# Expert mask in a transformer block: multiplied by GpSimd instead of added by selector matmuls

## The chip, the cores and the metric

One core of one Trainium2 chip runs the whole kernel in one launch. The metric is the device time of one execution, in microseconds (us). Lower is better. TensorE (PE) does matmuls, VectorE (DVE), ScalarE (ACT) and GpSimd (POOL) do the elementwise work, and SyncE (SP) issues all DMA transfers of this kernel.

## What is computed

For each of 4 sequences ("rows", `b`) of 1024 tokens with 256 features, the input is normalised per token (`xn`). Causal attention with 16 heads of 16 features, with rotary positions, and a feed-forward layer are both computed from `xn`, and both are added to the input. The feed-forward layer keeps, for each token, the 4 of 16 blocks of 64 hidden units that a router scores highest:

```python
prob = softmax(xf @ router_w.T + router_b)
_, idx = top_k(prob, 4)
mask = zeros((n, 16), bool).at[arange(n)[:, None], idx].set(True)
h = einsum('nd,ibd->nib', xf, w1b) + b1b
h = relu(where(mask[:, :, None], h, 0))
y = einsum('nib,dib->nd', h, w2b) + b2
return x + attention(xn) + y.reshape(x_shape)
```

## The kernel before

**Tiling.** Tokens lie in 8 tiles of 128 (`NT`), features in 2 blocks (`KB`), hidden units in 8 blocks of 128 (`FB`, each two router blocks). Attention runs in 16 groups of 4 heads (`GROUPS`, 4 for each row). A group has 48 "maxima" (a bfloat16 matmul of scores at L1065, whose maximum VectorE takes at L1333 and L1336), then 48 "scores" (L1124, with the causal triangle at L1127), whose exponentials ScalarE takes (L941), and 12 products with the values (`pv`, L1140). Maxima run about one group ahead of scores. GpSimd splits the maxima into three bfloat16 pieces (`split_maxima`, L832 to L841), TensorE transposes them (`maxT`, L1072), and SyncE places them through DRAM (`place_maxima`, L678 and L680) under the queries.

**The feed-forward layer.** It works on quarters of 256 tokens. For each hidden block, `hidden` runs two float32 matmuls (L1040, each recorded as two instructions) and a third, bfloat16 one (L1044). That third one multiplies a constant `sel` (-1e30 where a hidden unit belongs to a router block) by `unselT`, the transposed mask of blocks not chosen, so that ReLU on ScalarE (L932) with the bias gives zero there. `hT` holds one quarter, so the ReLU of the next quarter waits for the output tiles of this one. `ffn_tile` (L1053) multiplies `hT` by `w2` in two halves of four hidden blocks, and waits before each block, for even tiles, for ScalarE's count. VectorE adds the tile to `acc` (L1351). The mask comes from `route_logits` and `route_top` on VectorE, 8 transposes (L1032) and a copy (L1322).

**The order of work.** `arrange()` is a planner that runs when the kernel is built. It keeps a clock in TensorE columns, the moments when 7 PSUM banks come free, and costs of each work (`COST`, `READ`, `CHORE`, `POOL`). It lays out `ORDER` for TensorE, and from it the orders of ScalarE, VectorE and `POOL_ORDER` for GpSimd. Each engine runs its list strictly in order. `FIRST` is a fixed start for row 0. `group_work` says which feed-forward and projection works are spread over which group, in the order in which they must run, and a work that isn't due lets maxima or scores go first. GpSimd's list holds the rotations and splits into pieces of q and k (`CHAIN`: sin, cos, add, high, rest, mid, low; L786 to L814), the splits of maxima (which go first), the normalising of x (L820) and the addition of biases (L847).

**SyncE's queue** is written out by hand: loads of inputs, stores of pieces (L632, L639, L655), loads of "stacks" of pieces for a group (L647, L669), placements of maxima, stores and loads of attention outputs (L690, L701), and stores of results. A wait in it holds all that stands behind it.

**The last output weights.** The last group of the last row isn't sent over DRAM: `last_out` (L1112) multiplies `o_norm` by `wo_last`, the output weights of 4 heads laid 32 partitions apart, which four DMAs (L709) put into a buffer that VectorE set to zero (L1420).

## Time and profile before

| | |
|---|---|
| time, median of 3 runs | 830.44 us (830.43 to 831.54) |
| time of the profiled execution | 829.97 us |
| its span in the trace | 828.1 us |
| TensorE busy | 809.9 us, 98% |
| VectorE busy | 579.3 us, 70% |
| ScalarE busy | 426.2 us, 51% |
| GpSimd busy | 281.5 us, 34% |
| data moved by DMA | 81.9 MB, mean 99 GB/s |

The span runs from the first to the last instruction of the trace; the time of the execution includes what lies around it. Busy time of TensorE has overlaps merged: matmuls are pipelined, so the duration of one is longer than the distance between the starts of two. Releasers in brackets are inferred from semaphores. "L12" is line 12 of the kernel.

### The profile page before, as it was taken

Reading aid. Unit: us, or ns where it says so; the run is one execution under the profiler, and the core shown is the slowest. Engines: PE = TensorE matmul, PEld = TensorE weight load, DVE = VectorE, ACT = ScalarE, POOL = GpSimd, SP = SyncE. Lnnn points to the kernel's source line nnn. Section 1 sums busy time; section 2 is a strip of 40 time slices with the busy share of each in tenths; the row PEclk is TensorE's granted clock in tenths of the full one; section 3 lists DMA queues with packets and bytes.
Section 4 is the critical chain, followed back from the end, with each engine's and each line's share of the span. In section 5 each row is a group of like instructions: output and inputs, shape, how many; then the busy total and the mean of one; then the engine's idle time right before and its main releaser. Section 6 shows DMA issues by size and latency. Waiting matters only on the chain.

```text
span 828.1 us, 14880 instructions
## 1 busy us (share of the span) xinstructions
PE 809.9 (98%) x5278; PEld 492.0 (59%) x5278; DVE 579.3 (70%) x1799; ACT 426.2 (51%) x1018; POOL 281.5 (34%) x299
## 2 busy tenths in 40 slices
PE   5999999999999999999999999999999999999998
PEld 3677454544556655656656556664766556465764
DVE  6969877777998767576786856667676776767312
ACT  2523545665645645555464554645465464546552
POOL 3495149343650159067041028508400002000000
PEclk9999999999999999999999999999999999999999
DMA  8862515232524354141333315232060425000011
GB/s 273 243 186 77 169 53 166 92 90 92 147 73 125 94 142 151 43 118 39 87 133 74 95 53 166 91 91 92 2 215 4 109 61 142 15 15 16 15 58 51
DMA packets 53335, 81.91 MB, mean 99 GB/s; under 512 B 6796, under 2 KB 22092, under 8 KB 53260
## 3 DMA queue, kind: packets, MB, share of 16 engines
q1 hardware_dynamic: 53260, 80.95, 32.2%
q8 instruction: 42, 0.69, 0.4%
q14 instruction: 33, 0.27, 0.1%
HBM read 43.06 MB, written 37.88 MB: 98 GB/s over the span
## 4 chain that ended last, share of the span: by engine, by line
PE 92%; DVE 4%; ACT 2%; issue 1%; DMA 1%; SPq 0%; ACTq 0%; DVEq 0%
PE o_bank L1140 16%; PE banks L1065 14%; PE banks L1124 14%; PE banks L1040 14%; PE banks L1053 14%; PE banks L1014 7%; PE banks L1127 3%; PE banks L1023 3%; PE banks L1092 3%; PE banks L1044 2%; ACT probs L941 2%; DVE part_max L1333 1%; PE banks L1004 1%; DVE o_norm L1370 1%; DVE o_bank L1363 1%
## 5 line engine op out<-in xcount | busy, mean ns | idle before, releaser
L941 ACT ACTIVATE probs<-banks 128x512 f32<-128x512 f32 (+3 forms) x768 | 328.0, 496 | 244.0 <-PE banks L1127 174.5
L1124 PE MATMUL banks<-q_st,k_st 99*128 99x512 bf16 (+3 forms) x768 | 234.7, 327 | 2.6 <-ACT probs L941 1.0
L1065 PE MATMUL banks<-k_st,q_st 96*128 96x512 bf16 (+3 forms) x768 | 228.7, 327 | 0.7 <-DVE part_max L1333 0.2
L1336 DVE CUSTOM_DVE_ANT_0 banks<-banks,tri,part_max 128x512 f32<-128x512 f32 (+3 forms) x256 | 129.0, 555 | 68.3 <-PE banks L1065 68.0
L1333 DVE TENSOR_REDUCE part_max<-banks 128x1 f32<-128x512 f32 x256 | 160.1, 679 | 17.6 <-PE banks L1065 17.1
L1336 DVE CUSTOM_DVE_ANT_0 banks<-banks,tri 128x512 f32<-128x512 f32 (+3 forms) x256 | 120.1, 516 | 34.3 <-PE banks L1065 33.4
L832 POOL TENSOR_SCALAR max_neg<-row_max 128x16 f32<-128x16 f32 x32 | 8.1, 253 | 382.6 <-DVE row_max L1336 382.6
L1040 PE MATMUL banks<-xnT,w_sb 128*128 128x256 f32 x512 | 134.5, 386 | 0.1
L1140 PE MATMUL o_bank<-probs,v_sb 128*17 128x512 f32 (+3 forms) x1536 | 133.2, 487 | 0.7 <-DVE o_norm L1370 0.7
L1053 PE MATMUL banks<-w_sb,hT 128*128 128x256 f32 x512 | 121.2, 383 | 0.0
L1065 PEld LDWEIGHTS banks<-k_st,q_st 96*128 96x128 bf16 x768 | 73.3, 98 | 73.9 <-issue 19.9
L1124 PEld LDWEIGHTS banks<-q_st,k_st 99*128 99x128 bf16 x768 | 74.6, 97 | 61.4 <-ACT probs L941 18.1
L1127 PE MATMUL banks<-identb,tri 128*128 128x128 bf16 x512 | 108.1, 219 | 0.0
L1053 PEld LDWEIGHTS banks<-w_sb,hT 128*128 128x128 f32 x512 | 94.5, 190 | 16.7 <-ACT rope_sb L918 0.4
L1040 PEld LDWEIGHTS banks<-xnT,w_sb 128*128 128x128 f32 x512 | 90.7, 189 | 23.1 <-issue 2.8
L932 ACT ACTIVATE hT<-banks,b_sb 128x256 f32<-128x256 f32 x128 | 60.6, 474 | 81.7 <-PE banks L1044 68.7
L1140 PEld LDWEIGHTS o_bank<-probs,v_sb 128*17 128x17 f32 x1536 | 40.4, 97 | 87.0 <-issue 65.4
L1336 DVE DVE_READ_ACCUMULATOR2_ANT row_max<- 128x1 f32 x512 | 72.2, 141 | 0.0
L1127 PEld LDWEIGHTS banks<-identb,tri 128*128 128x128 bf16 x512 | 50.3, 98 | 18.8 <-issue 0.7
L1363 DVE STREAM_TRANSPOSE o_bank<-o_bank 128x512 f32<-128x512 f32 x31 | 22.7, 734 | 41.4 <-PE o_bank L1140 41.3
L1351 DVE TENSOR_TENSOR acc<-acc,banks 128x256 f32<-128x256 f32 x32 | 13.5, 421 | 46.2 <-PE banks L1053 46.2
L786 POOL TENSOR_TENSOR rope_sb<-rope_sb,sin_sb 128x1024 f32<-128x1024 f32 x14 | 33.0, 2357 | 34.7 <-DVE rope_sb L1272 34.7
(97 smaller groups left out, 732.5 us busy)
## 6 DMA issues: line engine op xcount, KB each, us to landing
term_scratch<-pieces SPq DMA_DIRECT2D x84, 256.0 KB, 2.9
q_st<-term_scratch SPq DMA_DIRECT2D x16, 768.0 KB, 5.9
k_st<-term_scratch SPq DMA_DIRECT2D x16, 768.0 KB, 8.3
y_scratch<-o_norm SPq DMA_DIRECT2D x31, 256.0 KB, 2.0
acc<-in_x SPq DMA_DIRECT2D x8, 512.0 KB, 3.9
rope_sb<-y_scratch SPq DMA_DIRECT2D x15, 256.0 KB
out<-acc SPq DMA_DIRECT2D x7, 512.0 KB, 2.9
x_sb<-in_x SPq DMA_DIRECT2D x3, 1024.0 KB, 5.8
```

The lines of the kernel that those rows point to most:

```text
L786: nc.gpsimd.tensor_tensor(y2, y2, sin_sb[:], ALU.mult).then_inc(rotated, 1)
L932: nc.scalar.activation(hT[:, m, :], filled("hid", b, q, m)[:, 0:QTR], ACT.Relu, bias=b1_sb[:, m:m + 1]).then_inc(s_out, 1)
L941: nc.scalar.activation(probs[:, h, PROBS_AT[u]:PROBS_AT[u] + w], filled("score", n, k, h)[:, 0:w], ACT.Exp, scale=SCALE).then_inc(s_out, 1)
L1014: last = nc.tensor.matmul(bank, w[:, k, mb * P:(mb + 1) * P], xnT[:, b % 2, k, c * HALF:(c + 1) * HALF], start=(k == 0), stop=(k == KB - 1))
L1040: nc.tensor.matmul(bank[:, 0:QTR], w1_sb[:, k, m * P:(m + 1) * P], xnT[:, b % 2, k, tokens], start=(k == 0), stop=False)
L1053: last = nc.tensor.matmul(bank[:, 0:D], hT[:, m, t % 2 * P:(t % 2 + 1) * P], w2_sb[:, m, :], start=(m == 0), stop=(m == FB - 1))
L1065: nc.tensor.matmul(bank[:, 0:w], q_st[0:KROWS, at, h, i * P:(i + 1) * P], k_st[0:KROWS, at, h, c * HALF:c * HALF + w], start=True, stop=Tr ...
L1124: last = nc.tensor.matmul(bank[:, 0:w], k_st[0:SROWS, at, h, j * P:(j + 1) * P], q_st[0:SROWS, at, h, q0:q0 + w], start=True, stop=not dia ...
L1127: last = nc.tensor.matmul(bank[:, 0:P], tri_k, identb[:], start=False, stop=True)
L1140: last = nc.tensor.matmul(o_bank[h * OW:h * OW + VW, q0:HALF], v_sb[:, b % 2, j, g * GH + h, :], probs[:, h, PROBS_AT[u]:PROBS_AT[u] + HAL ...
L1333: ins = nc.vector.tensor_reduce(part_max[:, h, at:at + 1], bank[:, 0:w], AX.X, ALU.max)
L1336: ins = nc.vector.tensor_tensor_reduce(bank[:, 0:w], bank[:, 0:w], tri[:, HALF - w:HALF], 1.0, least, ALU.add, ALU.max, to)
```

## The change

The selector matmul and its constant go. The mask is now that of the chosen blocks (1 or 0), transposed by the same 8 transposes (`chosenT`), copied by VectorE and stored to DRAM (`store_chosen`). `load_gates` reads it back for a quarter by two DMAs, each spreading 8 rows of the mask over 64 partitions, into `gates`, double buffered. After each two hidden blocks GpSimd multiplies the ReLU's output in place by the gates (`gate`), 64 times in all. `ffn_tile` waits for that instead of for ScalarE. The planner gets the cost of a gate (2700 columns), gives it priority behind the splits of maxima, and orders an output tile only when its gates are done by its clock. The first rotations of row 0 move from a fixed place into the planner's list. In SyncE's queue the stores and loads of gates are put between others. `wo_last` becomes one array, built beforehand, that is loaded into `x_sb`, the input buffer, after the last row's transposes.

```diff
-COST = {"hid": 2 * 4 * QTR + QTR, ...
+COST = {"hid": 2 * 4 * QTR, ...
...
+GATED, GATES = 500, 20000
+POOL = {"gate": 2700, "split": 3600, ...
...
-            todo = min(able, key=lambda todo: todo[1][0] != "split")
+            todo = min(able, key=lambda todo: ("split", "gate").index(todo[1][0]) if todo[1][0] in ("split", "gate") else 2)
...
+    def work_ready(what):
+        return what[0] != "ffn" or gated.get((what[1], what[2] // 2, 2 * what[3] + 1), clock + 1) <= clock
+
     def do_work(works):
         what = works.pop(0)
+        while not work_ready(what):
+            clock += 50
+            pump()
...
+        if what[0] == "chosenT":
+            gates[what[1]] = ready["vector"] + GATES
+        elif what[0] == "hid" and what[3] % 2:
+            pool_work(max(ready["scalar"], gates.get(what[1], 0)), ("gate", what[1], what[2], what[3] // 2))
...
-    pool_work(clock + 40000, *((step, 0, r) for r in (2, 3) for step in CHAIN[3:]))
+    pool_free = clock
+    pool_work(clock, *((step, 0, r) for r in (2, 3) for step in CHAIN[:3]))
+    pool_work(clock + 15000, *((step, 0, r) for r in (2, 3) for step in CHAIN[3:]))
...
-                may_work = works and may_fill(works[0][0])
+                may_work = works and may_fill(works[0][0]) and work_ready(works[0])
...
+            def store_chosen(b):
+                if b >= 2:
+                    for buffer in range(2):
+                        sp.wait_ge(gates_in[buffer], (b - 1) * 2 * 32)
+                sp.wait_ge(m_out, M_COUNT["chosenT", b])
+                sp.dma_start(gate_scratch[b % 2], chosenT[:]).then_inc(chosen_out, 16)
+
+            def load_gates(b, q):
+                if b or q >= 2:
+                    sp.wait_ge(gated, (b * 4 + q - 1) * FB // 2)
+                if q == 0:
+                    sp.wait_ge(chosen_out, (b + 1) * 16)
+                tokens = slice(q * QTR, (q + 1) * QTR)
+                for i in range(2):
+                    rows = gate_scratch[b % 2].rearrange("(m i) t -> i m t", i=2)[i, :, tokens]
+                    sp.dma_start(gates[i * 64:(i + 1) * 64, q % 2], rows.partition_broadcast(64)).then_inc(
+                        gates_in[q % 2], 16)
...
-            for h in range(GH):
-                d = (H - GH + h) * HD
-                sp.dma_start(wo_last[h * OW:h * OW + HD, :], woT[d:d + HD, :]).then_inc(wo_last_in, 16)
             load_x(1)
             store_first_pieces(0)
             store_first_pieces(1)
             load_first_stack()
+            store_chosen(0)
+            load_gates(0, 0)
+            load_gates(0, 1)
             store_other_pieces(0)
             store_other_pieces(1)
             load_stacks(1)
             place_maxima(0, 0)
+            load_gates(0, 2)
             store_pieces(0, 2)
             for b in range(B):
...
                 place_maxima(n, 1)
                 if b == 0:
+                    load_gates(0, 3)
...
                 place_maxima(n + 1, 0)
                 if b:
+                    store_chosen(b)
+                    load_gates(b, 0)
+                    load_gates(b, 1)
                     store_out(b - 1, 0)
...
+                elif not more:
+                    sp.wait_ge(s_out, S_COUNT["xnT", B - 1, NT // 2 - 1])
+                    sp.dma_start(wo_last, wo_last_c).then_inc(wo_last_in, 16)
                 place_maxima(n + 1, 1)
+                if b:
+                    load_gates(b, 2)
...
                 place_maxima(n + 2, 1)
+                if b:
+                    load_gates(b, 3)
...
+            def gate(b, q, pair):
+                pool.wait_ge(s_out, S_COUNT["hid", b, q, 2 * pair + 1])
+                if pair == 0:
+                    pool.wait_ge(gates_in[q % 2], (b * 2 + q // 2 + 1) * 32)
+                blocks = slice(2 * pair, 2 * pair + 2)
+                nc.gpsimd.tensor_tensor(hT[:, blocks, :], hT[:, blocks, :], gates[:, q % 2, blocks, :],
+                                        ALU.mult).then_inc(gated, 1)
...
-                if q == 0 and m == 0:
-                    pe.wait_ge(m_out, M_COUNT["unselT", b])
-                nc.tensor.matmul(bank[:, 0:QTR], sel[:, m, :], unselT[:, tokens], start=False,
-                                 stop=True).then_inc(s_fill, 1)
...
-                    if t % 2 == 0:
-                        pe.wait_ge(s_out, S_COUNT["hid", b, t // 2, m])
+                    if t % 2 == 0 and m % 2 == 0:
+                        pe.wait_ge(gated, (b * 4 + t // 2) * FB // 2 + m // 2 + 1)
```

## Rows read from the trace of the kernel before

**Rows 1.** The page: busy us and share of each engine; the chain by engine.
```profile
PE 809.9 (98%) x5278; PEld 492.0 (59%) x5278; DVE 579.3 (70%) x1799; ACT 426.2 (51%) x1018; POOL 281.5 (34%) x299
...
PE 92%; DVE 4%; ACT 2%; issue 1%; DMA 1%; SPq 0%; ACTq 0%; DVEq 0%
```
**Rows 2.** Windows: length, busy us of PE, PEld, DVE, ACT, POOL; clock, DMA share, GB/s.
```profile
0.00:50.00 50.00, 40.62 (x171) 28.17 (x172) 36.70 (x125) 19.86 (x46) 24.65 (x14) 1.00 0.83 259
50.00:100.00 50.00, 49.47 (x284) 32.88 (x281) 43.05 (x147) 19.92 (x46) 22.85 (x27) 1.00 0.44 128
100.00:200.00 100.00, 98.10 (x645) 49.15 (x644) 76.82 (x228) 55.23 (x127) 53.94 (x49) 1.00 0.34 105
...
300.00:400.00 100.00, 99.87 (x650) 61.10 (x649) 66.22 (x190) 51.05 (x117) 56.10 (x48) 1.00 0.30 91
```
**Rows 3.** A selector matmul and its successor in time: start, us, line.
```profile
61.12 0.27 PE L1044 MATMUL banks<-unselT,sel 128*128 128x256 bf16 x1
61.23 0.81 PE L1065 MATMUL banks<-k_st,q_st 96*128 96x512 bf16 x3
```
**Rows 4.** GpSimd's operations by line: ns min/median/max; or busy us, mean ns.
```profile
L786 POOL TENSOR_TENSOR rope_sb<-rope_sb,sin_sb x14: 2346/2356/2375, 43.0 to 574.3; 128x1024 f32<-128x1024 f32 x14
...
L808 POOL TENSOR_TENSOR rope_sb<-rope_sb,pieces 128x1024 f32<-128x1024 f32 x14 | 29.8, 2132 | 1.1
...
L820 POOL TENSOR_SCALAR x_sb<-x_sb,mv,rstd 128x256 f32<-128x256 f32 x24 | 28.9, 1220 | 38.1 <-DVE rstd L1251 38.1
```
**Rows 5.** L1044's waits (us, times); DMAs to landing, the last is L678's.
```profile
  DVE unselT L1322: 2.1, 3
...
k_st<-term_scratch SPq DMA_DIRECT2D x16, 768.0 KB, 8.3
...
acc<-in_x SPq DMA_DIRECT2D x8, 512.0 KB, 3.9
...
DMA to landing us min/median/max: 1.3/1.8/5.3
```
**Rows 6.** Ends of two quarters, all engines, in order of time.
```profile
425.58 9.65 POOL L820 TENSOR_SCALAR x_sb<-x_sb,mv,rstd 128x256 f32<-128x256 f32 x8 [20.03 <-DVE rstd L1251]
...
433.55 0.47 ACT L932 ACTIVATE hT<-banks,b_sb 128x256 f32<-128x256 f32 x1 [0.30 <-PE banks L1044]
...
436.08 1.94 PE L1053 MATMUL banks<-w_sb,hT 128*128 128x256 f32 x8
...
796.65 0.53 ACT L932 ACTIVATE hT<-banks,b_sb 128x256 f32<-128x256 f32 x1
...
797.02 3.62 PE L1053 MATMUL banks<-w_sb,hT 128*128 128x256 f32 x16
```
**Rows 7.** The start of the first quarter's output, all engines, in time.
```profile
37.83 0.68 DVE L1322 COPY unselT<-banks 16x1024 bf16<-16x1024 bf16 x1 [0.42 <-PE banks L1032]
...
38.69 0.27 PE L1044 MATMUL banks<-unselT,sel 128*128 128x256 bf16 x1
...
43.00 2.36 POOL L786 TENSOR_TENSOR rope_sb<-rope_sb,sin_sb 128x1024 f32<-128x1024 f32 x1
...
45.63 1.03 PE L1065 MATMUL banks<-k_st,q_st 96*128 96x512 bf16 x4
...
46.16 0.70 DVE L1336 CUSTOM_DVE_ANT_0 banks<-banks,tri 128x512 f32<-128x512 f32 x1 [5.15 <-PE banks L1065]
...
46.49 1.89 PE L1053 MATMUL banks<-w_sb,hT 128*128 128x256 f32 x8
```
**Rows 8.** Row 1: a placing of maxima on SyncE; the first output tile.
```profile
266.91 0.73 SPq L680 DMA_DIRECT2D q_st<-max_scratch  x1
...
301.20 1.99 PE L1053 MATMUL banks<-w_sb,hT 128*128 128x256 f32 x8
```
**Rows 9.** VectorE's cosine product beside a GpSimd copy, in time.
```profile
25.23 0.41 POOL L857 COPY o_norm<-bv_sb 128x256 f32<-128x256 f32 x1
...
25.30 0.88 DVE L1281 TENSOR_TENSOR rope_sb<-rope_sb,cos_sb 128x512 f32<-128x512 f32 x1
```

More of the change, by code:

```diff
@@ L206 @@
 SPLIT, PLACE = 1200, 16000
-POOL = {"split": 3600, "sin": 5640, "cos": 5640, "add": 5640, "high": 2500, "rest": 5100, "mid": 2500,
+GATED, GATES = 500, 20000
+POOL = {"gate": 2700, "split": 3600, "sin": 5640, "cos": 5640, "add": 5640, "high": 2500, "rest": 5100, "mid": 2500,
         "low": 5100, "xn": 1580, "bias": 5700}
@@ L246, in pump @@
                 split[todo[1][1:]] = pool_free + SPLIT
+            elif todo[1][0] == "gate":
+                gated[todo[1][1:]] = pool_free + GATED
     def engine_of(kind):
@@ L323, in do_work @@
                 do_max()
-            order.append(works.pop(0))
+            what = works.pop(0)
+            while not work_ready(what):
+                clock += 50
+                pump()
+            order.append(what)
             clock += COST["ffn"]
             read(what, at, READ["ffn"])
+            wide = True
             return 2 * COST["ffn"]
         read(what, fill(what, COST[what[0]]), READ[what[0]])
+        if what[0] == "chosenT":
+            gates[what[1]] = ready["vector"] + GATES
+        elif what[0] == "hid" and what[3] % 2:
+            pool_work(max(ready["scalar"], gates.get(what[1], 0)), ("gate", what[1], what[2], what[3] // 2))
         if what[0] == "out" and what[1] + 1 < B and what[2] % 2:
@@ L392, in arrange @@
             do_max()
-        elif works:
+        elif works and work_ready(works[0]):
             do_work(works)
@@ L489, in block_kernel @@
         tri_k = tri[:, HALF - P:HALF]
[L490 removed]
+        gates = sb("gates", [P, 2, FB, QTR], BF16)
         pieces = sb("pieces", [P, 2, NPIECE, T], BF16)
@@ L1039, in hidden @@
                 for k in range(KB):
-                    nc.tensor.matmul(bank[:, 0:QTR], w1_sb[:, k, m * P:(m + 1) * P], xnT[:, b % 2, k, tokens],
-                                     start=(k == 0), stop=False)
-                if q == 0 and m == 0:
-                    pe.wait_ge(m_out, M_COUNT["unselT", b])
-                nc.tensor.matmul(bank[:, 0:QTR], sel[:, m, :], unselT[:, tokens], start=False,
-                                 stop=True).then_inc(s_fill, 1)
+                    last = nc.tensor.matmul(bank[:, 0:QTR], w1_sb[:, k, m * P:(m + 1) * P], xnT[:, b % 2, k, tokens],
+                                            start=(k == 0), stop=(k == KB - 1))
+                last.then_inc(s_fill, 1)
             def ffn_tile(b, t, part):
@@ L1108, in last_out @@
                 if i == 0:
-                    pe.wait_ge(wo_last_in, 16 * GH)
+                    pe.wait_ge(wo_last_in, 16)
                 if i % 2 == 0:
                     pe.wait_ge(normed, 2 * GROUPS + i // 2)
-                nc.tensor.matmul(banks[:, BANK["outl", t], 0:D], o_norm[:, 1, i * P:(i + 1) * P], wo_last[:], start=False,
+                nc.tensor.matmul(banks[:, BANK["outl", t], 0:D], o_norm[:, 1, i * P:(i + 1) * P], wo_last, start=False,
                                  stop=True).then_inc(m_fill, 1)
```

110 lines of the change are left out of this document (53 added, 57 removed).

## Prediction

> **What bounds the kernel now.** I read the busy shares first: TensorE is busy 98% of the span, VectorE 70%, ScalarE 51% and GpSimd 34%, and the chain of work that ended last is 92% TensorE [rows 1]. The windows say where this holds: TensorE is busy 49.5 of 50 us from 50 to 100 us, and 98.1 to 99.9 of every 100 us from 100 to 800 us (the two ends of these seven are shown); only the first 50 us (40.6 busy) and the tail are thinner [rows 2]. The granted clock is 1.00 in all of them, which is the 2.4 GHz level. So nearly every column taken off TensorE after 50 us is time taken off the end, unless its instructions begin to wait for somebody. The other engines have room over a stretch: GpSimd is busy 56 of 100 us in its fullest window, though VectorE has little between 50 and 100 us (43 of 50) [rows 2].
>
> One execution is what I can add up: its span is 828.1 us, and its time was 829.97, so 1.9 us lie around the span. The median of the three runs is 830.44, 0.5 us above it.
>
> **Selector matmuls removed.** There are 128 of them. The 0.27 us that the trace gives one is not its price, because matmuls overlap in the pipeline. The order of time shows it: a selector starts at 61.12 and its successor at 61.23 [rows 3], and so it is for nearly all. That is 0.11 us each; 256 columns at 2.4 GHz are 0.107. 128 x 0.109 = 13.9 us. In 3 places TensorE also waited for the copy of the transposed mask, 2.1 us together [rows 5]; part of this overlaps weight loads, and I count 0.5. Together -14.4 us. The selector's weight load lies under the matmul in front of it and gives nothing. The bracket is 13.7 (columns alone) to 16.0 (all of the wait as well).
>
> **Gate multiplications added on GpSimd.** There are 64, each over 128x512, float32 by bfloat16 into float32. The nearest rows are the subtraction of a bfloat16 piece, 2.13 us for 1024 columns, and the sine product, 2.36 [rows 4]. Their halves are 1.07 and 1.18; with some fixed part I take 1.16. The high end is the scalar-pair operation, 1.22 us for 256 columns [rows 4], which would make 2.44. 64 x 1.16 = 74 us, so GpSimd goes from 281 to about 355 us of 815. As throughput this costs nothing; as a relay between ScalarE and TensorE it can.
>
> How late is each quarter's relay? In 16 quarters of hidden layers, the second half of the first output tile needs the last hidden block. In row 1, quarter 3, the last ReLU ends at 434.02 and the second half starts at 436.08, 2.1 us later [rows 6]. In the last quarter the ReLU ends at 797.18, and eight matmuls of 0.216 after 797.02 the second half starts, 1.6 us later [rows 6]. Read in the same way the distance is 1.6 to 2.8 us in 11 quarters and 7 to 19 in five. (The first half needs only block 3 and had 4.1 us or more.) The new path takes a hand-over from ScalarE and one to TensorE, some 0.24 together (from the mask copy's end at 38.51 to the matmul at 38.69 it was 0.18 [rows 7], and between dependent GpSimd steps 0.06), and the gate's 1.16: 1.4 us. With GpSimd free that fits, and the planner orders an output tile only when its gates are due. With GpSimd inside a rotation step it must wait up to 2.36 us [rows 4]. Laid over the old times, GpSimd is in the last of eight normalising steps until 435.23 in row 1, quarter 3 [rows 6], so a gate would end at 436.4 and the half be 0.5 us late; row 0, quarter 1 would be 1.6 late by a rotation step in the same way, and quarter 2 of rows 1 and 2 would just fit. Since the order moves, I price four such meetings by their mean excess over 0.7 us of slack: 3 x 1.65x1.65/(2x2.36) = 1.7, and 0.1 for the shorter step. I take +2; the bracket is 0 to 6.
>
> **Start-up, the one place where the relay is exposed.** Today the hidden blocks of quarter 0 end at 45.63, four maxima follow, and the first output tile starts at 46.49 [rows 7]. After the change the blocks end at about 44.8. The transposed mask is ready at 38.5 [rows 7]; its store of 32 KB should land like the maxima's store of 12 KB (1.3 to 5.3 us, median 1.8 [rows 5]), at 40.5. Then come the broadcast loads, 512 KB a quarter in rows of 512 bytes. The trace has none; bounds are the acc load of the same size (3.9 us) and the k_st load (8.3 for 768 KB) [rows 5], so they land at 44.9 to 49.3. I take 46, near the lower row, as the size is its own. GpSimd is held until 43.00 by the bias additions and until 45.4 by one rotation step [rows 7]. Two gates from 46 end at 48.3, the first half starts at 48.5, and its second half waits 0.6 us more for the fourth gate. TensorE meanwhile has about 12 maxima (1.9 us of columns; VectorE needs 0.70 us for a wide one [rows 7], so they can't come faster). Idle: 48.5 - 44.8 - 1.9 = 1.8, + 0.6 = 2.4; if a second rotation step goes first, 2.35 more. I take +3, bracket 1.2 to 7.5. This isn't recovered, because TensorE is full from there on and the work is the same.
>
> **SyncE's queue.** Four issues for the last output weights and one for the selector go; 4 stores and 32 loads come, at 0.3 to 0.8 us each. Behind the first five of them stand the 12 stores of the other heads and the stack of group 1, some 4.5 us later than now; the first maxima of group 1 come after all 48 of group 0, each of which takes VectorE 0.3 to 0.9 us, so the cover is some 20 us and nothing is charged. In row 1 the first gates stand behind the placing of maxima, which ends at 267.64, so they land near 275; the first output tile is at 301.20 [rows 8]: 26 us of cover, and GpSimd, which must stand at its first gate until then, had nothing else in its list before 287. A later quarter's load waits for the gates two quarters back, which then come a group's part earlier; behind it stand a stack and a placing that have ten us or more. Cost 0. The extra 16 x 512 KB = 8.4 MB find the DMA engines at a third of their time [rows 2]: 0.
>
> **Last output weights.** They are loaded once, ready-made, into a buffer free since the last transposes, long before their use in the last matmuls. The four head loads and a memset near the start leave, where VectorE waits for x anyway. 0 at both ends.
>
> **GpSimd beside VectorE.** A row shows that they can slow each other: VectorE's cosine product took 0.88 us at 25.30, where a GpSimd copy ran from 25.23 to 25.64 [rows 9], and 0.68 the other three times. It reads two SBUF tensors. In the long middle VectorE reads PSUM with at most one SBUF operand, and GpSimd's 14 sine products took 2346 to 2375 ns whatever VectorE did [rows 4]. So 0. The Trainium skill (GPSIMD Engine Reference, Key points) says that GpSimd shares its SBUF interfaces with VectorE, with contention for VectorE instructions in a 2-port mode or with two SBUF inputs. The trace agrees with both halves of this, and by that rule moving work to GpSimd would cost only in the routing and first rotations, under 1 us here.
>
> **Sum.** 828.1 - 14.4 + 2 + 3 = 818.7 of span, + 1.9 = 820.6. The planner lays the whole order anew; the stretches of 100 us differ in TensorE's idle time by 1.8 us (98.10 to 99.87 [rows 2]), so I give the order -1 to +3 and round to 821.
>
> **Rivals.** (1) *The relay is the new bound, slower than before.* If a gate takes g us, start-up costs 3 + 4(g - 1.16), the ten tight quarters past it (median distance 2.1) cost g + 0.24 - 2.1 each once positive, and the four meetings 2 in sum and 0.8 each more for each us of g above 1.16. At g = 2.44 this is 8.1 + 5.8 + 2 + 4 x 1.0 = about 20, so 829.97 - 14.4 + 20 = 836. It decides from g of about 2.1. For it speaks the scalar-pair row; against it both tensor-pair rows [rows 4]. Chance 0.08. (2) *TensorE's freed time becomes waiting.* VectorE has 43 of 50 us between 50 and 100 [rows 2], GpSimd's splits of maxima now stand behind gates and rotations, and placements arrive later; half or more of the gain goes: 826 to 831, say 828. Against it: from 300 to 400 us TensorE lacks only 0.13 us of its window with VectorE at 66 and ScalarE at 51 [rows 2]. Chance 0.14. (3) *The clock falls in the start-up gap.* The granted clock stayed 1.00 in the first window, where TensorE lacks 9.4 us [rows 2], but no gap of 2 to 5 us after its start exists in this trace. Were the following 5 us at 1.2 GHz, they would deliver half their columns: +2.5, 823.5; with 10 us, +5. The Trainium skill (TensorE: Matmul & The Clock Gate, the part on the clock gate) has the clock depend on how busy TensorE was lately, halved when idle; by it this is possible, and maxima every 0.7 us speak against. Chance 0.06. (4) *The change does not do what it says*, the selectors' columns being hidden: then 830. The starts in [rows 3] nearly exclude this; 0.02.
>
> **How the numbers follow.** The forecast, 821 (815.5 to 826), has 0.70. Low end: 829.97 - 16.0 + 1.2 = 815.2; high: all brackets' upper halves, 826. The range of 8 in 10 takes in rival 3 and most of rival 2: 815 to 829. A measurement here can tell about 0.2% (1.7 us) from no change. Rival 2 splits into 0.09 faster, 0.04 within and 0.01 slower. Faster: 0.70 + 0.06 + 0.09 = 0.85; within: 0.04 + 0.02 = 0.06; slower: 0.08 + 0.01 = 0.09.
>
> **What would show it.** The selector's line is gone, and a hidden block's fourth matmul is followed by its successor after 0.22 us. Gates take 1.1 to 1.2 us. The first output tile starts between 48 and 50, with VectorE's maxima undisturbed. Waits of TensorE for GpSimd appear at quarter ends, under 6 us in sum, with the clock at 1.00. I am wrong if gates take over 2 us, if the first tile starts after 53, or if waits for maxima or their placing grow.

## The result, and the profile after

The changed kernel takes 835.5 us (median of four, 833.7 to 836.3) against 830.9 for the kernel before on the same chip: 1.0054 of its time, with a 95% interval of 1.0042 to 1.0066. I had forecast 821, between 815 and 829. It is slower by 4.5 us where I expected 9.4 less, so 14 us are to be found. The four executions fall in two pairs: 833.7 and 834.8 with a mean granted clock of 0.996, and 836.2 and 836.3 with 0.992; the traced one, from which all rows of this kernel come, is one of the slower pair.

From the page of the changed kernel: busy time of each engine, the chain that ended last by engine, and two groups (busy us, mean ns of one | idle time before them and what ended it).

```profile
PE 807.0 (97%) x5150; PEld 483.2 (58%) x5150; DVE 580.4 (70%) x1798; ACT 424.8 (51%) x1018; POOL 352.9 (42%) x362
PE 88%; ACT 4%; DVE 3%; DMA 2%; POOL 1%; issue 1%; SPq 0%; DVEq 0%; ACTq 0%; POOLq 0%
L877 POOL TENSOR_TENSOR hT<-hT,gates 128x512 f32<-128x512 f32 x64 | 73.7, 1156 | 207.9 <-ACT hT L993 141.1
L1111 PE MATMUL banks<-w_sb,hT 128*128 128x256 f32 x512 | 124.9, 389 | 6.7 <-POOL hT L877 6.7
```

The gates (L877) came out as forecast: 64 of 1.156 us. TensorE still has 88% of the chain, but it had 92 [rows 1], and the difference went to waits and to DMA. The windows say where, against [rows 2]:

```profile
core 0: us, PE busy (x) PEld busy (x) DVE busy (x) ACT busy (x) POOL busy (x), PEclk, DMA share, GB/s
0.00:50.00 50.00, 38.95 (x153) 26.39 (x153) 36.99 (x127) 19.86 (x46) 19.17 (x11) 1.00 0.76 227
50.00:100.00 50.00, 45.66 (x245) 31.77 (x246) 36.46 (x129) 15.22 (x36) 37.52 (x37) 0.90 0.54 146
100.00:200.00 100.00, 96.32 (x599) 48.88 (x597) 76.36 (x216) 54.53 (x126) 55.80 (x53) 0.98 0.38 112
300.00:400.00 100.00, 99.30 (x618) 57.02 (x617) 65.75 (x184) 50.90 (x118) 66.14 (x51) 1.00 0.36 112
```

TensorE's busy time from 50 to 100 us fell from 49.5 to 45.7 and the granted clock from 1.00 to 0.90, so even of the busy time a part ran at half rate. From 100 to 200 a smaller loss of both kinds follows. From 200 us on it is 98.5 to 99.6 of every 100, a little under before.

The start in order of time (start us, us, engine line op out<-in xcount [idle before <-what ended it]):

```profile
36.62 0.59 SPq L671 DMA_DIRECT2D q_st<-term_scratch  x1
38.46 0.32 SPq L671 DMA_DIRECT2D k_st<-term_scratch  x1
38.65 0.68 DVE L1380 COPY chosenT<-banks 16x1024 bf16<-16x1024 bf16 x1 [0.42 <-PE banks L1093]
39.36 0.32 SPq L714 DMA_DIRECT2D gate_scratch<-chosenT  x1
...
45.64 1.68 PE L1123 MATMUL banks<-k_st,q_st 96*128 96x512 bf16 x8
45.77 2.70 SPq L725 DMA_DIRECT2D gates<-gate_scratch  x4
...
48.93 0.28 PE L1123 MATMUL banks<-k_st,q_st 96*128 96x256 bf16 x1 [0.36 <-DVE row_max L1394]
...
52.82 4.49 POOL L877 TENSOR_TENSOR hT<-hT,gates 128x512 f32<-128x512 f32 x4 [6.66 <-DMA gates<-gate_scratch]
...
54.12 3.75 PE L1111 MATMUL banks<-w_sb,hT 128*128 128x256 f32 x8 [4.90 <-POOL hT L877]
...
58.12 0.43 DVE L1394 CUSTOM_DVE_ANT_0 banks<-banks,tri 128x256 f32<-128x256 f32 x1 [6.04 <-PE banks L1123]
```

The mask left VectorE at 39.33 and its store was issued at 39.36. SyncE could issue the loads only when the store had landed, at 45.77: 6.4 us later. Their data released GpSimd at 52.82, 7.0 us later again. The first output tile began at 54.12, where it had begun at 46.49 [rows 7]. TensorE had issued the 11 maxima that its order has ahead of the first tile by 48.93, the last of them at the pace at which VectorE frees banks, and then stood for 4.9 us. VectorE, with nothing new in the banks, stood for 6.04. In windows of 2 us over the same place (columns as above) one sees what the standing did to the clock:

```profile
46.00:48.00 2.00, 1.61 (x9) 0.58 (x6) 1.83 (x5) 0.23 (x1) 0.16 (x1) 1.00 0.12 33
48.00:50.00 2.00, 0.57 (x2) 0.19 (x2) 2.00 (x9) 0.00 (x0) 0.00 (x0) 0.92 0.43 115
50.00:52.00 2.00, 0.00 (x0) 0.00 (x0) 2.00 (x10) 0.00 (x0) 0.00 (x0) 0.50 1.06 209
52.00:54.00 2.00, 0.00 (x0) 0.00 (x0) 0.08 (x2) 0.00 (x0) 1.18 (x2) 0.50 1.17 262
54.00:56.00 2.00, 1.88 (x5) 1.54 (x6) 0.00 (x0) 0.00 (x0) 2.00 (x2) 0.50 1.07 343
56.00:58.00 2.00, 2.00 (x7) 1.44 (x6) 0.00 (x0) 0.00 (x0) 2.00 (x3) 0.50 1.01 308
58.00:60.00 2.00, 2.00 (x7) 1.56 (x6) 0.49 (x2) 0.00 (x0) 1.61 (x1) 0.52 0.15 41
60.00:62.00 2.00, 2.00 (x13) 1.70 (x12) 1.18 (x7) 0.00 (x0) 0.00 (x0) 1.00 0.68 179
```

The granted clock went to 0.50, the 1.2 GHz level, from about 49.7 (the window from 48 to 50 has 0.92) to 60 us. TensorE had been busy 2.2 of the 4 us from 46 to 50 and its last maximum had ended at 49.21, so the clock fell within 0.5 us of the gap's start. Six of those ten microseconds were work at half rate, some 3 us of time (my estimate from these rows). A second, smaller case follows in row 0's last quarter: the last gate stood behind six normalisations of x on GpSimd.

```profile
109.12 7.23 POOL L884 TENSOR_SCALAR x_sb<-x_sb,mv,rstd 128x256 f32<-128x256 f32 x6
116.32 1.15 POOL L877 TENSOR_TENSOR hT<-hT,gates 128x512 f32<-128x512 f32 x1
117.52 0.83 PE L1111 MATMUL banks<-w_sb,hT 128*128 128x256 f32 x2 [1.80 <-POOL hT L877]
```

```profile
116.00:118.00 2.00, 0.48 (x2) 0.45 (x3) 0.00 (x0) 0.00 (x0) 1.47 (x2) 0.99 0.00 0
118.00:120.00 2.00, 2.00 (x7) 1.00 (x6) 0.64 (x2) 0.00 (x0) 0.00 (x0) 0.50 0.00 0
```

### The profile page after: what moved, and what is told of

Its sections match the earlier page's. It is cut to its first block, busy times and chain, and to the rows that moved or that the text cites. A ratio compares the mean times of both kernels' runs of the same rounds, so it can differ in the third digit from the quotient of the medians.

```text
span 834.4 us, 14740 instructions
## 1 busy us (share of the span) xinstructions
PE 807.0 (97%) x5150; PEld 483.2 (58%) x5150; DVE 580.4 (70%) x1798; ACT 424.8 (51%) x1018; POOL 352.9 (42%) x362
## 4 chain that ended last, share of the span: by engine, by line
PE 88%; ACT 4%; DVE 3%; DMA 2%; POOL 1%; issue 1%; SPq 0%; DVEq 0%; ACTq 0%; POOLq 0%
PE o_bank L1198 15%; PE banks L1123 14%; PE banks L1182 14%; PE banks L1111 14%; PE banks L1101 13%; PE banks L1075 7%; PE banks L1084 3%; PE banks L1185 3%; PE banks L1150 3%; ACT probs L1002 3%; POOL x_sb L884 1%; DMA gate_scratch<-chosenT 1%; DMA gates<-gate_scratch 1%; PE banks L1065 1%; DVE banks L1394 1%
## 5 line engine op out<-in xcount | busy, mean ns | idle before, releaser
L1123 PE MATMUL banks<-k_st,q_st 96*128 96x512 bf16 (+3 forms) x768 | 226.1, 328 | 1.6 <-DVE row_max L1394 1.2
L1394 DVE CUSTOM_DVE_ANT_0 banks<-banks,tri,part_max 128x512 f32<-128x512 f32 (+3 forms) x256 | 128.5, 554 | 57.7 <-PE banks L1123 57.4
L877 POOL TENSOR_TENSOR hT<-hT,gates 128x512 f32<-128x512 f32 x64 | 73.7, 1156 | 207.9 <-ACT hT L993 141.1
L1111 PE MATMUL banks<-w_sb,hT 128*128 128x256 f32 x512 | 124.9, 389 | 6.7 <-POOL hT L877 6.7
L1111 PEld LDWEIGHTS banks<-w_sb,hT 128*128 128x128 f32 x512 | 96.8, 194 | 24.6 <-issue 5.3
```

The costliest lines, as they stand in the source:

```text
L877: nc.gpsimd.tensor_tensor(hT[:, blocks, :], hT[:, blocks, :], gates[:, q % 2, blocks, :], ALU.mult).then_inc(gated, 1)
L1111: last = nc.tensor.matmul(bank[:, 0:D], hT[:, m, t % 2 * P:(t % 2 + 1) * P], w2_sb[:, m, :], start=(m == 0), stop=(m == FB - 1))
L1123: nc.tensor.matmul(bank[:, 0:w], q_st[0:KROWS, at, h, i * P:(i + 1) * P], k_st[0:KROWS, at, h, c * HALF:c * HALF + w], start=True, stop=Tr ...
L1394: ins = nc.vector.tensor_tensor_reduce(bank[:, 0:w], bank[:, 0:w], tri[:, HALF - w:HALF], 1.0, least, ALU.add, ALU.max, to)
```

## A table by stage

Waits of TensorE are too scattered for one row. So I took, from the start times of all matmuls in each trace, the time from each to its successor, and its excess over the columns at 2.4 GHz. The sums are cut at the first score of group 1: "start" is all up to there (with row 0's first three quarters of hidden layers), "rest" is groups 1 to 15. Times in us. The last column is the median of the timed runs.

```
kernel                            start  its excess   rest  its excess   median
before                            116.6     17.2     701.0    108.1      830.4
mask left out, order of before    114.4     17.5     689.9    107.7      817.6
mask left out, planner told       117.1     18.9     693.6    111.8      822.9
changed, tiles don't wait         120.4     23.6     695.9    115.2      828.7
changed, first masks constant     118.8     22.0     696.1    115.2      827.4
changed                           127.7     30.8     696.1    115.2      835.5
changed, clock kept up            125.8     29.0     696.1    115.0      833.3
changed, planner not told         126.7     29.8     693.3    112.6      832.2
changed, mask due later           125.4     28.6     694.7    113.5      831.6
selectors in row 0 (padded)       116.5     17.1     695.5    112.9      825.0
the same, three gates ahead       117.9     18.5     691.2    108.0      821.3
```

Start and rest come from one traced execution of each kernel, each about 1 us or less from its median: before and changed lie 6.2 us apart here and 5.1 in the last column. "Start" is good to about 1.4 us only, since the landing of the first inputs differs from one execution to the next (the last two kernels do the same work there), and the split into columns and excess to about 1 us. From before to changed, the start grew by 11.1 and the rest shrank by 4.9, where 13.7 us of columns went: the excess grew by 13.6 in the start and by 7.1 in the rest (with the columns these make 7.0 us, where start and rest make 6.2). The experiments below make the rows.

## Experiments

**What the removed matmuls are worth, and what the planner makes of it.** Both kernels leave the mask out of the feed-forward layer. The first keeps the order of before, the second also tells the planner that a hidden work has 2048 columns and no longer 2304.

```diff
-                                     start=(k == 0), stop=False)
...
-                nc.tensor.matmul(bank[:, 0:QTR], sel[:, m, :], unselT[:, tokens], start=False,
-                                 stop=True).then_inc(s_fill, 1)
+                                            start=(k == 0), stop=(k == KB - 1))
+                last.then_inc(s_fill, 1)
 # and in the second kernel
-COST = {"hid": 2 * 4 * QTR + QTR, ...
+COST = {"hid": 2 * 4 * QTR, ...
```

> The kernel before, in its own order, without the 128 selector matmuls; the mask is left out of the result, all blocks count. It prices the removed columns alone. If a selector column was full price (the prediction's step), this is 13 to 15 us faster than before, 816 to 817. If the columns were hidden behind waits, it is under 5 us faster. No relay, no gate loads, no new order here, so no theory of those expects a loss.

> The same, but the planner also knows that a hidden block costs 2048 columns instead of 2304, so it lays the order anew (mask left out again). Theory start-up (most of the loss of the change comes from its first 65 us): the same as the run without the new plan, within 2 us. Theory order (the new order is what costs, whatever the relay does): 5 to 8 us slower than that run.

Measured: 817.6 us (0.9843 of before [0.9828, 0.9857]) and 822.9 (0.9908 [0.9893, 0.9922]). The matmuls are worth 13 us, near the 14.4 of my sum. But the true cost in the planner takes 5.3 back with no mask, no gate and no new DMA in play, as the theory of the order had it. From "who waits for whom" (us, times, longest), first the order of before, then the new order; L1121 is the score, L1040 the hidden matmul, L1069 the transposing of maxima:

```profile
PEld banks L1121 <- ACT probs L941: 18.1, 57, 0.8
PEld banks L1040 <- ACT hT L932: 1.6, 5, 0.4
```

```profile
PEld banks L1121 <- ACT probs L941: 25.2, 77, 0.8
PEld banks L1040 <- ACT hT L932: 3.5, 8, 0.6
PEld banks L1069 <- POOL max_pc L841: 1.3, 1, 1.3
```

The hidden works now seem shorter, and the planner mixes maxima and scores differently. In the new order 178 scores follow another score with nothing but its triangle between them, where 156 did. Then the banks come free only as fast as ScalarE takes exponentials: these waits rose from 57 to 77 times. Score to score (with the triangle) has 11.8 us of excess in the first order and 16.3 in the second, in groups 0, 4, 5, 9 and 14 above all: 4.4 of the 5.3.

**The relay alone.** The changed kernel in its own order, but GpSimd writes its product to the gates' buffer and not to `hT`. The output tiles wait for ScalarE as before the change. The next quarter's first ReLU waits for the products, since they read `hT`; the trace has no wait of ScalarE for GpSimd there. The output lacks the mask.

```diff
-                nc.gpsimd.tensor_tensor(hT[:, blocks, :], hT[:, blocks, :], gates[:, q % 2, blocks, :],
+                nc.gpsimd.tensor_tensor(gates[:, q % 2, blocks, :], hT[:, blocks, :], gates[:, q % 2, blocks, :],
...
+                    act.wait_ge(gated, (b * 4 + q) * FB // 2)
...
-                    if t % 2 == 0 and m % 2 == 0:
-                        pe.wait_ge(gated, (b * 4 + t // 2) * FB // 2 + m // 2 + 1)
+                    if t % 2 == 0:
+                        pe.wait_ge(s_out, S_COUNT["hid", b, t // 2, m])
```

> The changed kernel, its order, its gate loads and its 64 GpSimd products all kept, but the products are written over the gates' own buffer and the output tiles wait for ScalarE as before (the mask is left out of the result; the next quarter's first ReLU waits for the products). This takes the relay away and nothing else. Theory start-up: TensorE's 5 us wait, the 2 us one at 115 us and the half clock go, 10 to 12 us faster than the change, 824 to 825.5, still 7 to 9 us slower than the columns alone, which is the order. Theory relay (waits of TensorE for GpSimd all along are the loss): all of it goes, 816 to 819. Theory load (GpSimd's and DMA's extra work slows others): no better than 833.

Measured: 828.7 us (0.9981 [0.9972, 0.9991]), outside the ranges of all three theories. So 6.8 of the changed kernel's us are TensorE's own waits for the gates with what they do to the clock. In the table all of it is in the start; the rest is equal to 0.2 us. The other 5.9 lie between this kernel and the one with the planner told. A part is the order that the change asks for, since TensorE runs the changed kernel's order here: the planner holds back output tiles until their gates are due. With no wait of TensorE for gates, the first tile is at 49.39 here and was at 46.49 [rows 7]. But this edit does not take the late gates away from GpSimd. It stood 6.69 us for their load, and its split of the maxima, which comes behind the four products and a rotation step in its list, ended at 60.60. TensorE waited 2.15 us for it at 60.66, and the clock was 0.50 for some 3.5 us from 62.0:

```profile
52.44 4.50 POOL L877 TENSOR_TENSOR gates<-hT,gates 128x512 bf16<-128x512 f32 x4 [6.69 <-DMA gates<-gate_scratch]
...
60.38 0.22 POOL L905 TENSOR_TENSOR max_pc<-max_rest,max_pc 128x16 bf16<-128x16 f32 x1
...
60.66 0.23 PE L1131 MATMUL banks<-identb,max_pc 128*128 128x128 bf16 x1 [2.15 <-POOL max_pc L905]
```

```profile
62.00:64.00 2.00, 2.00 (x6) 1.43 (x5) 1.75 (x3) 0.47 (x1) 2.00 (x2) 0.51 1.08 235
```

So 6.8 us is the least that the relay costs in the changed kernel, and 5.9 the most that is left for the order beyond the planner's true cost.

**The first masks without DMA.** The gates of row 0's first two quarters are set to 1 by a memset, so that GpSimd need not wait for their load; the rest is the changed kernel. Those quarters lack the mask.

> The changed kernel in which the gates of row 0, quarters 0 and 1, are not loaded: GpSimd sets both buffers to 1 while it is idle near the start, so these 512 tokens count all blocks. The mask of row 0 is stored as before and loaded from quarter 2 on. GpSimd's products, their order and TensorE's waits for them stay. Theory mask transfer (what is late at the start is the way over DRAM behind the stack loads): the first gate starts near 46.2 us instead of 52.8, the first tile near 48.7, the clock stays 1.00, and the run is 4 to 6 us faster than the change, 829.5 to 831.5. Theory GpSimd (the products and the rotation steps between them are the delay): the tile starts after 51 us and the run is at best 2 us faster.

Measured: 827.4 us (0.9958 [0.9944, 0.9973]), 8.1 below the changed kernel and below what I had expected, with the clock at 1.00 in the whole execution. All the excess saved lies in the start, the first gate starts at 46.08 and the split of the maxima ends at 57.7. The load of the first mask behind its store, with the clock that falls behind them, is the largest single piece. What is left against the kernel with the planner told is 4.5 us. The relay's wait of 1.8 us is still there, and here the clock stayed at 1.00 behind it:

```profile
110.56 1.13 PE L1114 MATMUL banks<-w_sb,hT 128*128 128x256 f32 x4 [1.80 <-POOL hT L878]
```

**The clock's part.** 22 small transposes into a bank that is free at this point, right before the first output tile, keep TensorE active while it waits.

```diff
                     pe.wait_ge(w2_in, 16)
+                    pe.wait_ge(pad_set, 5)
+                    for _ in range(22):
+                        nc.tensor.transpose(o_bank[:, 0:P], ident[:], ident[:])
```

> The changed kernel, with 22 float32 transposes of the identity into the attention's unused bank put just ahead of the first output tile, where TensorE stood idle from 49.1 to 54.1 us. They compute nothing of the result. Nothing in the waits gets shorter. Theory clock: the granted clock, which was 0.50 from about 50 to 60 us, stays 1.00, and since some 6 us of the work then ran at half speed, the run is 2.5 to 4 us faster than the change, 831.5 to 833. Theory gates alone: the stage is bound by the gates and by VectorE anyway and the clock costs nothing: 835.

Measured: 833.3 us (1.0035 [1.0024, 1.0047]), 2.2 less. The interval touches that of the changed kernel (1.0042 to 1.0066), so this alone is weak. The transposes don't bridge the whole gap: in the traced execution (834.4) the clock still fell, but for some 4 us instead of 10 (windows of 2 us of this kernel, columns as above).

```profile
50.00:52.00 2.00, 0.96 (x9) 0.72 (x7) 1.42 (x8) 0.00 (x0) 0.10 (x1) 1.00 1.19 224
52.00:54.00 2.00, 0.81 (x4) 0.68 (x4) 0.00 (x0) 0.00 (x0) 2.00 (x2) 1.00 1.12 288
54.00:56.00 2.00, 2.00 (x8) 1.32 (x7) 0.00 (x0) 0.00 (x0) 2.00 (x3) 0.65 1.04 352
56.00:58.00 2.00, 2.00 (x6) 1.63 (x6) 0.49 (x2) 0.00 (x0) 2.00 (x2) 0.50 0.73 213
58.00:60.00 2.00, 2.00 (x12) 1.66 (x11) 1.09 (x7) 0.00 (x0) 0.68 (x1) 0.99 0.29 31
```

The executions say more than the medians. Of this kernel, three with a mean clock of 1.000 took 832.5 to 833.2 us and three with 0.996 took 833.9 to 835.5; of the changed kernel, the two with 0.992 took 836.2 and 836.3. So the clock is worth some 3 us in the changed kernel's slower executions, by comparison and not by an edit that changes nothing else.

The Trainium skill (TensorE: Matmul & The Clock Gate, the part on HAM oscillation) says that a wait for DMA can drop the clock, so that work after the wait starts at half rate. The changed kernel's windows agree: the first 5.9 us of work behind a wait of 4.9 ran at 0.50. A gap of 1.8 us at 117.5 was also followed by a stretch at 0.50, and one of the same length in the kernel with constant masks wasn't. So the length of one gap doesn't tell here whether the clock falls.

**The planner's two figures for the mask.** In the first kernel the planner is not told that the hidden work is shorter; the second tells it that the gates are ready 33,000 columns after the mask and no longer 20,000, nearer to the measured landing.

> The changed kernel with one number of the planner put back: a hidden block costs 2304 columns as before the change, though it now takes 2048. Nothing that runs is added or removed, only the order moves. Theory order (the new order from the true cost lost 5.3 us in the run without selectors): 3 to 6 us faster than the change, 829.5 to 832.5, and the scores of groups 5 and 9 take 50.0 us again instead of 51.5. Theory relay: no difference, 834 to 837.

> The changed kernel whose planner counts 33000 columns (13.7 us) instead of 20000 (8.3 us) from the mask's copy to the gates, which is what the transfer took in the first row (39.3 to 52.8 us). The gates come no earlier, but more maxima stand ahead of the first tile, so VectorE, idle from 52 to 58 us in the change, goes on. Theory mis-sized transfer (the plan, not the wait, is at fault): 3 to 5 us faster than the change, 830.5 to 832.5. Theory unavoidable gap: TensorE has only maxima to do until the gates come, so the same idle time: 834 to 836.

Measured: 832.2 us (1.0022 [1.0013, 1.0032]) and 831.6 (1.0013 [1.0004, 1.0022]). Both give back some 3 to 4 us, as the theories of order and of the mis-sized transfer said, and neither gets under the kernel before. The true cost costs 3.3 here and 5.3 in the kernel without a mask, so the two losses don't simply add. With the old cost the rest has 112.6 of excess instead of 115.2, but a new spot appears: the excess is 1.6, 1.7 and 1.6 us larger in groups 6, 7 and 10 than in the same order without the mask.

The second kernel also shows how the clock falls without a long gap. TensorE never stood for more than 0.4 us from 46 to 50.9, but its maxima came one by one as VectorE freed banks, and at 50.9 the clock went to 0.50 for 10 us. The run is 3.9 us faster even so, with the clock low for as long as in the changed kernel, so its gain is not the clock's.

```profile
48.00:50.00 2.00, 0.89 (x4) 0.29 (x3) 2.00 (x9) 0.00 (x0) 2.00 (x1) 1.00 0.67 141
50.00:52.00 2.00, 1.46 (x5) 0.51 (x5) 2.00 (x11) 0.00 (x0) 2.00 (x2) 0.73 1.16 217
```

**Selectors kept for row 0.** If the start is the problem, row 0 can keep its selector matmuls and its old queue, and rows 1 to 3 take the gates, in the order of before.

```diff
+G0 = 1
...
-        elif what[0] == "hid" and what[3] % 2:
+        elif what[0] == "hid" and what[3] % 2 and what[1] >= G0:
...
+                if b < G0:
+                    if q == 0 and m == 0:
+                        pe.wait_ge(m_out, M_COUNT["chosenT", b])
+                    last = nc.tensor.matmul(bank[:, 0:QTR], sel[:, m, :], chosenT[:, tokens], start=False, stop=True)
```

> Row 0 keeps the selector matmuls (fed by the transposed mask of blocks not chosen, 16 partitions), the first rotations and SyncE's queue of the kernel before; rows 1 to 3 use GpSimd's gates; the planner keeps the old cost of a hidden block. All three causes are out of it: 24 x 4 = 96 selectors less, 10.4 us. If start-up and order are the whole loss: 819.5 to 822, 1.1% faster than before. If the relay costs in rows 1 to 3 too: above 824.

Measured: 831.7 us (1.0012 [1.0002, 1.0021]), a miss by 10 us. The trace had the cause in two rows, to be read beside [rows 3]:

```profile
61.97 0.28 PE L1108 MATMUL banks<-chosenT,gates 16*128 16x256 bf16 x1
62.18 1.04 PE L1131 MATMUL banks<-k_st,q_st 96*128 96x512 bf16 x4
```

My selectors read 16 rows ("16*128"), where those of the kernel before read 128 with zeros below. The successor comes 0.21 us later and not 0.11, and the selector itself follows the hidden matmul after 0.312 and not 0.216: 0.197 us for each of 32. Two kernels test this: the same with padded selectors, and the kernel before with narrow ones (two slices changed, `sel[0:NBLK, m, :], unselT[0:NBLK, tokens]`).

> The kernel with selectors in row 0 only and the mask multiplied by GpSimd in rows 1 to 3, in the order of the kernel before, again, with one difference: its 32 selector matmuls read all 128 rows (16 of data, the rest zero), as those of the kernel before do, where the last version read 16. In the last version's trace each narrow selector took 0.210 us to its successor instead of 0.109, and came 0.312 us behind the hidden matmul instead of 0.216: 0.197 us for each of 32, 6.3 us. Theory (the matmuls over 16 rows were the unexplained loss, the rest of that version is sound): 831.7 - 6.3 = 825.4 us. Rival (the loss is in the relay of rows 1 to 3): 831 to 832 us, as before.

> The kernel before with its 128 selector matmuls reading 16 rows of the selectors and of the mask instead of 128 (the other 112 are zero). Theory (a matmul over 16 rows between matmuls over 128 costs 0.197 us more at its two changes of rows, as in the version with selectors in row 0): 128 x 0.197 = 25 us longer, 856 us. Rival (the 0.197 us came from where that version kept its selectors, in the buffer of the gates): 830 to 831 us.

Measured: 825.0 us (0.9934 [0.9919, 0.9948]) and 855.5 (two executions; 1.0302 [1.0282, 1.0323]), both within 0.5 us of the forecast. 128 narrow selectors cost 25 us. The padded version is faster than the kernel before and than the changed one, by 5.6 and 10.5 us, and its start is that of the kernel before, 116.5 of 116.6.

**The relay in rows 1 to 3.** What stays against the kernel without the mask is 3.4 us of row 0's selectors (32 x 0.107) and 4.0 more. Their place was groups 6, 7 and 10.

> The version with the padded selectors in row 0, with the planner's allowance from a multiplication's due end to the tile that reads it at 4.0 us instead of 0.5. With the order of before kept, the relay showed waits of about 1.5 us inside a feed-forward pair in groups 6, 7 and 10, where a multiplication stands behind a rotation on GpSimd. Theory (these waits are real and a later tile takes them away at no cost): 3 to 5 us below the padded version, 820.5 to 822.5 us, which beats both kernels. Rival (moving the tiles later pushes the order into other waits, as telling the true cost did, +5.3): 825 us or more.

Measured: 825.0 us (0.9937 [0.9920, 0.9953]). This kernel says nothing on the question: the planner, given the later due time, laid out exactly the same order, since it had the tiles late enough already. It shows how well two equal kernels agree. So the order on GpSimd was changed by hand:

```diff
 ORDER, BANK, BEFORE, POOL_ORDER = arrange()
+for what, places in ((("gate", 1, 2, 3), 1), (("gate", 1, 3, 3), 2), (("gate", 2, 2, 3), 1)):
+    at = POOL_ORDER.index(what)
+    POOL_ORDER.insert(at - places, POOL_ORDER.pop(at))
```

> The version with padded selectors in row 0, with three of GpSimd's 48 multiplications moved ahead in its own order: the last of quarter 2 in rows 1 and 2 by one operation (ahead of the second operation of a rotation's split), the last of quarter 3 in row 1 by two (ahead of two of the next row's normalisations). The last run with later tiles in the plan came out with the same order of work as the padded version, so it told nothing of this. Theory (the relay's price in rows 1 to 3 is that these three stand behind other work on GpSimd: 1.5, 0.95 and 1.5 us inside the feed-forward pairs of groups 6, 7 and 10): 825.0 - 4.0 = 821.0 us, between 820.5 and 822. Rival (the wait is for the ReLU or for the semaphore, wherever the multiplication stands): 824.5 to 825.5 us.

Measured: 821.3 us (0.9886 [0.9870, 0.9903]). The same place in both kernels, first with the gate behind a piece of the split, then ahead of it:

```profile
382.47 0.48 ACT L996 ACTIVATE hT<-banks,b_sb 128x256 f32<-128x256 f32 x1 [0.19 <-PE banks L1104]
...
384.05 2.12 POOL L861 TENSOR_TENSOR rope_sb<-rope_sb,pieces 128x1024 f32<-128x1024 f32 x1
...
386.13 1.15 POOL L875 TENSOR_TENSOR hT<-hT,gates 128x512 f32<-128x512 f32 x1
...
387.34 1.13 PE L1120 MATMUL banks<-w_sb,hT 128*128 128x256 f32 x4 [1.35 <-POOL hT L875]
```

```profile
383.75 0.47 ACT L999 ACTIVATE hT<-banks,b_sb 128x256 f32<-128x256 f32 x1 [0.19 <-PE banks L1107]
...
385.15 1.15 POOL L878 TENSOR_TENSOR hT<-hT,gates 128x512 f32<-128x512 f32 x1
...
386.18 1.94 PE L1123 MATMUL banks<-w_sb,hT 128*128 128x256 f32 x8
```

The ReLU ends at 382.95 in the first, and the gate, 1.15 us of work, starts 3.2 us later, since GpSimd's list has the split's next step, begun at 384.05, ahead of it. One place ahead, the gate starts 0.9 us after the ReLU and the tile runs through. The three moves give 3.7 us, all that the relay cost in rows 1 to 3 (excess of the rest: 112.9 to 108.0, where it is 107.7 without any mask). With these gates ahead of GpSimd's other work, the relay costs nothing in rows 1 to 3 that these runs can tell (0.3 us of excess), and this version is the fastest of all kernels here that leave nothing out.

**The last output weights.** The kernel before with this part of the change alone: one transfer of ready-made weights onto row 3's inputs, in place of four loads and a memset.

> The kernel before with only the last output weights moved onto the place of row 3's inputs, filled by one transfer late in the program. Theory (this part costs nothing, as forecast): within 0.2% of the kernel before, 829.5 to 831.5 us. Rival (it gives or costs part of the change's time): outside of that, by 2 us or more.

Measured: 830.3 us (0.9999 [0.9989, 1.0008]). Nothing, as forecast.

## Why the prediction was wrong

The direction was wrong: 4.5 us slower, not 9.4 faster. Term by term:

- *Selectors, -14.4:* right in mechanism, a little large. 13.0 measured with nothing else changed, just under the columns' 13.7 that were my lower end; the 0.5 us of waiting was not gained.
- *The gate's duration, 1.16:* right, 1.156. Rival 1, which needed gates over 2.1 us, is out.
- *Start-up, +3 (1.2 to 7.5):* this step failed. The mechanism was the one I described, with its pieces mis-sized. I took the store at the median of the maxima's stores, 1.8 us, though it goes out behind two stack loads of 768 KB (2.7 and 0.9 us behind); it landed after 6.4, where the other three stores of a mask took 1.6 to 1.7. I took 5.5 us from there to the gates' landing; it was 7.0, and no load of gates in the trace landed in under 5.0 us (median 6.1). The tile came at 54.12 and not 48.5, past the point at which I said I would be wrong. In place of an idle time of 2.4 us TensorE stood 4.9 at a stretch, ran up to the gap with maxima at VectorE's pace, and the clock went to 1.2 GHz for 10 us. Taking the load away gave 8.1 us, clock included; 2 to 3 of these are the clock's by the kernel with transposes. The rows I had (1.3 to 5.3 for the small store) didn't hold the case, and I took the middle of them where the queue was at its fullest. That the loads in front held the store up is read from the times, for no run sends it ahead of them.
- *Rival 3, the clock:* it came true, priced at 2.5 to 5 us with a chance of 0.06. Its chance hung on the start-up term: with a gap of 2.4 us I gave it little, the real gap was twice as long. The second reason was wrong in itself. I held that maxima every 0.7 us speak against a fall; in the kernel with the mask due later the clock fell while such maxima ran.
- *The relay in the steady state, +2 (0 to 6):* the mechanism was right, down to the meeting with the normalisations and with the rotations. In the order of before it costs 3.7 to 4 us; in the changed kernel's order, one case of 1.8 us at 117.5 with its fall of the clock. Quarter 2 of rows 1 and 2, which I had as just fitting, was late by some 1.5 us.
- *The order, -1 to +3:* the second step that failed. I read the size of this term from how much one stretch of the old order differs from another. It isn't a spread: the planner, told a true and smaller cost, gave a worse order by 5.3 us, and the order with the gates' due times another 2.7 to 5.9: 5.9 with GpSimd still held by the load, 4.5 with constant masks, of which 1.8 are the relay's wait. Rival 2 (the freed time becomes waiting) was priced too low, 826 to 831, and had the mechanism in part: scores that wait for ScalarE and, at 60.66 in the kernel whose tiles don't wait, a split of maxima behind gates; not VectorE's load from 50 to 100 us or late placements.
- *SyncE's queue, DMA bandwidth in the long run, the last weights, GpSimd beside VectorE:* nothing seen, as forecast. The changed kernel's windows from 200 us on leave little room for them. The queue's cover depends on the order, though: in the kernel with the mask due later TensorE waited 2.37 us for a placing of maxima at 70.7.

The range was narrower than its own terms: their dear ends add up to 829.97 - 13.7 + 6 + 7.5 + 3 = 833, and I stopped at 829. By the first path below, three of the four terms (selectors, start-up, order) came out beyond their dear ends.

Along one path: 817.6 without the mask; +4.0 for gates in rows 1 to 3 (825.0 less 3.4 of row 0's selectors); +10.6 for gates in row 0, with their places in the queue and the later rotations (to 832.2); +3.3 for the true cost in the planner: 835.5. Along the other path: 817.6, +5.3 planner, +5.9 due times with all the new work but the relay, +6.8 TensorE's waits for gates; or, by way of the constant masks, +5.3, +4.5, +8.1. The parts depend on each other, so neither list is the one true split. Against my sum, the first path has the selectors worth 1.5 us less, the relay 2 dearer, the start-up 7.6 and the order 2.9 beyond the 0.4 that I had rounded up for it; with 0.5 between the profiled execution and the median before, these are the 14.5 us from 821 to 835.5. What stays open is how the 5.9 divide between tiles held back, maxima put in their place, and the wait at 60.66 with its clock; I made no kernel that has the one without the others.

## What to carry to other kernels

A step that is moved onto another engine has its price at the place where the pipeline is shortest, here the start, where nothing covers a round trip over DRAM; price its transfers by what stands in the queues at that very moment, not by a median, and where TensorE thins out for several us, by a gap or by matmuls that come one by one, price the clock with it. An operation that others wait for goes ahead of the long, patient work on its engine: three moves by one or two places were worth 3.7 us. And an order planned by costs is itself a part of the kernel: a truer cost made it worse by 5 us, so measure a change of the work with the order held, then the order.

## What the runs showed of the hardware that I had not expected

- A matmul that reads 16 rows, between matmuls that read 96 or 128, cost 0.197 us more than one of the same columns that reads 128 rows: 25 us for 128 of them. The Trainium skill (TensorEngine Tiling (Array Packing), Key Properties) says that a change of the tiling mode drains TensorE; the runs agree, with 0.1 us at each side of the narrow matmul. The kernel before pays it too, in its last 10 us: its float32 matmuls over 64 rows (L1103) alternate with ones over 128, and all of them start 0.31 to 0.32 us apart, where the same 256 columns take 0.216 elsewhere.
- A 32 KB store issued 2.7 and 0.9 us behind two stack loads of 768 KB took 6.4 us to land, 0.2 us after the second of them; the other three of the same size took 1.6 to 1.7.
- The granted clock fell to 0.50 within 0.5 us of the start of a gap of 4.9 us, and stayed there for 10 us, of which TensorE worked 5.9. It fell for 3.5 us behind a gap of 1.8 us in the changed kernel and stayed at 1.00 behind one in the kernel with constant masks. And it fell at 50.9 us in the kernel with the mask due later, where no gap had been over 0.4 us and TensorE was busy 0.89 of the 2 us before 50; with constant masks it was busy 0.85 of the same 2 us and the clock stayed.
